# GpSimd's memsets and one weight split moved behind the layer norm in a six-block transformer kernel

## What is computed

```python
def _layernorm(x, axis=-1, eps=1e-05):
    m = jnp.mean(x, axis=axis, keepdims=True)
    v = jnp.var(x, axis=axis, keepdims=True)
    return (x - m) / jnp.sqrt(v + eps)
...
    x = x + _L0_xattn_ref(_layernorm(x, axis=-1), ctx_4096, L0_xattn_Wq, L0_xattn_Wk, L0_xattn_Wv, L0_xattn_Wo)
    x = x + _L0_attn_ref(_layernorm(x, axis=-1), L0_attn_w_q, L0_attn_w_k, L0_attn_w_v, L0_attn_w_out)
    x = x + _L0_ffn_ref(_layernorm(x, axis=-1), L0_ffn_route_w, L0_ffn_A, L0_ffn_Bw)
    x = x + _L1_xattn_ref(_layernorm(x, axis=-1), ctx_4096, ctx_4096, L1_xattn_Wq, L1_xattn_Wk, L1_xattn_Wv, L1_xattn_Wo)
    x = x + _L1_attn_ref(_layernorm(x, axis=-1), L1_attn_Wq, L1_attn_Wk, L1_attn_Wv, L1_attn_Wo, L1_attn_cos, L1_attn_sin)
    x = x + _L1_ffn_ref(_layernorm(x, axis=-1), L1_ffn_rmsnorm_weight, L1_ffn_Wg, L1_ffn_Wu, L1_ffn_Wd)
```

## Time and profile before

| what | value |
|---|---|
| median of three runs | 2087.39 us |
| the profiled execution's own time | 2098.17 us |
| its span | 2096.8 us |
| TensorE busy | 1927.6 us (92%) |
| VectorE busy | 1292.1 us (62%) |
| ScalarE busy | 860.1 us (41%) |
| GpSimd busy | 546.6 us (26%) |
| mean DMA rate | 124 GB/s |

### The profile page before, as it was taken

How to read it: one execution, slowest core, us unless ns; L and a number is a source line. 1 busy time by engine, 2 the same in 40 slices (tenths; PEclk the granted TensorE clock), 3 DMA queues, 4 the chain that set the end, 5 groups by cost and what they waited for, 6 DMA issues and landing times.

```text
span 2096.8 us, 29638 instructions
## 1 busy us (share of the span) xinstructions
PE 1927.6 (92%) x11932; PEld 1414.5 (67%) x11932; DVE 1292.1 (62%) x1608; ACT 860.1 (41%) x1409; POOL 546.6 (26%) x264
## 2 busy tenths in 40 slices
PE   7899999999997999999998996989999999978977
PEld 5799999999996778787776874623333333366833
DVE  3445454454444788889976755757777774266465
ACT  2211111111113666665664451146777777535421
POOL 0000000000001555564510001046777777410000
PEclk9999999999998999999999998879999999999889
DMA  5543433343326656666625426523434320135052
GB/s 178 169 119 94 126 98 113 99 124 92 86 76 169 212 189 199 189 204 207 223 89 152 161 72 180 112 75 79 99 79 91 87 59 1 41 121 219 1 190 74
DMA packets 154808, 259.30 MB, mean 124 GB/s; under 512 B 36477, under 2 KB 102321, under 8 KB 147505
## 3 DMA queue, kind: packets, MB, share of 16 engines
q1 hardware_dynamic: 154673, 257.42, 41.3%
HBM read 192.39 MB, written 61.76 MB: 121 GB/s over the span
## 4 chain that ended last, share of the span: by engine, by line
PE 81%; DVE 10%; ACT 3%; DMA 2%; issue 2%; SPq 0%; POOL 0%; ACTq 0%; DVEq 0%
PE psum L475 10%; PE psum L1720 7%; PE psum L1737 5%; PE psum L456 4%; PE psum L458 4%; PE psum L457 4%; PE psum L443 3%; PE psum L285 3%; PE psum L286 3%; PE psum L287 3%; PE psum L1753 3%; PE psum L816 3%; DVE top L1913 3%; PE psum L817 3%; PE psum L818 3%; PE psum L831 3%
## 5 line engine op out<-in xcount | busy, mean ns | idle before, releaser
L1913 DVE TENSOR_REDUCE top<-psum 128x4 f32<-128x2048 f32 (+1 forms) x146 | 294.0, 2026 | 103.2 <-PE psum L1701 102.9
L1983 POOL TENSOR_TENSOR added<-probs_f 128x1024 f32<-128x1024 f32 x126 | 299.1, 2376 | 181.5 <-ACT probs_f L1838 133.7
L1838 ACT ACTIVATE probs_f<-psum 128x512 f32<-128x512 f32 x512 | 278.5, 594 | 142.0 <-PE psum L1720 129.7
L608 DVE TENSOR_REDUCE top<-psum 128x2 f32<-128x512 f32 x272 | 186.5, 692 | 198.0 <-PE psum L443 197.8
L907 DVE TENSOR_TENSOR probs_low<-probs,probs_high 128x1024 fp32r<-128x1024 f32 x136 | 197.7, 1458 | 77.7 <-ACT probs L870 77.5
L869 ACT ACTIVATE probs_high<-psum 128x1024 fp32r<-128x1024 f32 x136 | 139.9, 1029 | 164.1 <-PE psum L818 151.6
L1720 PE MATMUL psum<-q_rows,k_rows 97*128 97x512 f32 x512 | 197.7, 462 | 3.1 <-DMA q_rows<-t_high 2.4
L1720 PEld LDWEIGHTS psum<-q_rows,k_rows 97*128 97x128 f32 x512 | 80.9, 191 | 174.1 <-ACT probs_f L1838 159.0
L456 PE MATMUL psum<-c_high,w_high 128*128 128x256 f32 (+1 forms) x672 | 190.7, 284 | 3.2 <-issue 3.2
L457 PE MATMUL psum<-c_low,w_high 128*128 128x256 f32 (+1 forms) x672 | 190.6, 284 | 0.0
L458 PE MATMUL psum<-c_high,w_low 128*128 128x256 f32 (+1 forms) x672 | 190.5, 284 | 0.0
(11 more groups left out here) (359 smaller groups left out, 3820.2 us busy)
## 6 DMA issues: line engine op xcount, KB each, us to landing
wf_rows<-in_ffn_w_dram SPq DMA_DIRECT2D x42, 512.0 KB, 4.4
staged<-in_ctxT_dram SPq DMA_DIRECT2D x32, 512.0 KB, 4.7
k_four<-k_high SPq DMA_DIRECT2D x128, 128.0 KB, 3.4
wf_rows<-in_ffn_w_dram SPq DMA_DIRECT2D x8, 1376.0 KB, 7.9
q_dram<-wf_turned SPq DMA_DIRECT2D x42, 256.0 KB, 2.3
gate_up<-q_dram SPq DMA_DIRECT2D x10, 1024.0 KB, 8.1
value_high<-v_high SPq DMA_DIRECT2D x32, 256.0 KB, 3.7
value_low<-v_low SPq DMA_DIRECT2D x32, 256.0 KB, 4.6
```

The source lines that it names most:

```text
L608: dve.tensor_reduce(top0[:, r0:r0 + 2, n], psum[:, bank, :].rearrange("p (i n) -> p i n", i=2), AX_X, ALU.max).then_inc(*b.bank_read.up())
L1838: act.activation(probs[:, n % 6, half * BANK:(half + 1) * BANK], psum[:, half, :], ACT.Exp, scale=scale).then_inc(*f.exped.up())
L1913: dve.tensor_reduce(top1[:, first:end, t, chunk], psum[:, MAXIMA + first:MAXIMA + end, :], AX_X, ALU.max).then_inc(*f.max_read.up())
L1983: pool.tensor_tensor(added[pair % 4][:], probs[:, n % 6, :], probs[:, (n + 1) % 6, :], ALU.add).then_inc(*f.added.up())
```

## The change

dve_output leaves out its split at the last unit. In both causal stages VectorE makes that split directly behind the layer norm instead, ahead of the low parts of xnT: unit 3 of the query weights (unit 19 of the stream) in d, unit 1 (57) in g. These are the only two places where the left-out step did something. GpSimd's memsets in the causal stages and in the second cross attention wait for the norm's end (xn_set) in place of the last addition to x (x_added). No instruction is added or removed.

```diff
--- before.py
+++ after.py
@@ -311,12 +311,13 @@
                     act_split(u0 + u + ahead)
 
         def dve_output(u0, per, ahead, upto, banks):
+
             for u in range(2 * per):
                 if u % per == per - 1:
                     dve.wait_ge(*s.unit_read.at(u0 + u + 1))
                     for t in range(TT):
                         dve_add_to_x(u // per, t, banks[TT * (u // per) + t])
-                if u0 + u + ahead < upto:
+                if u0 + u + ahead < upto and u < 2 * per - 1:
                     dve_split(u0 + u + ahead)
 
 
@@ -1403,6 +1404,7 @@
                     done.then_inc(*f.o_set.up())
 
                 dve_layernorm(norm, [xn[:, t, :] for t in range(TT)])
+                dve_split(u_q + (3 if ahead == 4 else 1))
                 for i in range(KT // 2):
                     dve.wait_ge(*f.xnT_high_set.at(i + 1))
                     dve.tensor_tensor(xnT_low[:, 2 * i:2 * i + 2, :], bank_pair(4 + i),
@@ -1469,7 +1471,7 @@
 
             def gpsimd_program():
                 wait_pool()
-                pool.wait_ge(*s.x_added.at(before))
+                pool.wait_ge(*s.xn_set.at(norm))
                 pool.memset(qz[:], 0.0).then_inc(*f.zeroed.up())
 
             def sync_program():
@@ -1970,7 +1972,7 @@
                     pool.tensor_tensor(oT_low[:, kv, :], o_raw[:], oT_high[:, kv, :].bitcast(F32),
                                        ALU.subtract).then_inc(*f.o_split.up())
 
-                pool.wait_ge(*s.x_added.at(before))
+                pool.wait_ge(*s.xn_set.at(4))
                 pool.memset(ones[:], 1.0).then_inc(*f.ones_set.up())
                 for k in k_rows:
                     pool.wait_ge(*f.ones_set.now())
```

## The result

| | before | changed |
|---|---|---|
| median of six runs, us | 2088.04 | 2077.64 |
| lowest to highest | 2086.55 to 2093.22 | 2074.64 to 2079.01 |
| the profiled execution, us | 2098.17 | 2078.95 |

The ratio is 0.9944, with a 95% interval of 0.9930 to 0.9958: 11.7 us faster, between 8.8 and 14.6 (the medians by themselves lie 10.4 apart). The forecast was 13.2 us and 2074.2.

What follows compares the result with a forecast made beforehand. TensorE bounds the kernel (81% of the chain), idling behind three norms; memsets' 11.17 us and splits' 2.00 make 13.16, rounded to 13.2 off 2087.39: 2074.2 us, range 2071.0 to 2079.5.

Steps and rivals of the forecast that it cites:

- The stalls: In three norms, L172 and L188 held by GpSimd memsets; moving these removes 1.35, 5.06 and 4.76 us, 11.17 together.
- the sum of 13.16 us: Excess from last L303 to first transpose: 2.34 us in d, 5.06 in second cross attention, 5.76 in g.
- four ends: L172 (three norms) and L188 (second cross attention) each end with a GpSimd memset, agreeing within 0.03 us.
- The division of the sum: Of the gain at the norms, 11.17 us came from the memsets and 2.00 from the splits in d and g.
- The moved split: Behind the norm in d and g, 1.21 us fits VectorE's idle 1.84, leaving 0.6; cost nothing.
- The first rival: In d and g the memset holds the moved split, giving back up to 2.9 and 6.3 us: 2083.4; chance 0.04.
- The mask: In g it lands later, ScalarE waits 2 us at L1286; covered with 1.7 us to spare, cost zero.
- The fourth rival: In d and g a very late mask makes ScalarE keep high parts from TensorE: 2091.9 or slower; chance 0.02.
- The panels of the query projection: In the second cross attention two weight panels land before TensorE's transposes end, covered by 0.7 us.
- The second rival: Query projection panels land late, taking at most the second cross attention's 5.06 us: 2079.3; chance 0.05.
- The clock: TensorE still restarts at half clock behind the three norms, after idle times of about 6.15 us; net cost taken as zero.
- The range's 3 and 4 us: Allowance for TensorE's half clock behind restarts: about 3 us below the forecast and 4 above.

Runs made afterwards that it cites:

- the last kernel: Changed kernel plus tables ahead of the last panel, one projection split ahead of the additions, 25 unread matmuls before each norm's wait, 45 before feed-forward: 2070.83 us, ratio 0.9879.
- the two kernels with fillers: Changed kernel with unread TensorE matmuls before the norms' waits: 40 each, ratio 0.9964; 25 each, 45 before feed-forward, plus two order edits, ratio 0.9879.

## Why the prediction was right, point by point

- The stalls. L172 and L188 at 0.17 us in all norms, 4.06 or 4.07 us from L303 to L208 in each stage: the sum of 13.16 us stands in the trace as 13.17. That the memset is the cause was argued from four ends and is now shown: the memsets alone bring 5.07 us in the second cross attention and 1.34 and 4.77 in the others, the split alone lengthens L172 to the same end.
- The division of the sum. The prediction gave 2.00 us to the splits as a part of its own. Alone they are worth nothing. It should have read the split as a step in front of a fixed end: where a wait for something else lies behind it, taking it away only lengthens the wait.
- The moved split. 1.22 us beside the memset, with 0.70 us of VectorE's wait left, as worked out (0.6). The first rival fell; the run with a reading GpSimd operation shows when it would have been right.
- The mask. A new wait of ScalarE of 3.26 us in g, against the 2 worked out, since the mask landed 6.1 us after its issue and not 4.5. TensorE asked for its fourth unit 12.4 us behind its restart, not 11.5, because it ran at half clock for longer, so the margin was 1.2 us, against 1.7. The term stays at nothing. The fourth rival fell.
- The panels of the query projection. No wait in the changed kernel (0.69, released by ScalarE). The second rival was near all the same: with 1.7 us off the transposes and the LoRA stage 2.9 us shorter, so that the panels go out later against the norm, the panel is what TensorE waits for, by 3.15.
- The clock. "The new idle times are all about 6.15 us" was off for the second cross attention, 5.14, because TensorE's last product there ends later against VectorE's additions; the rows of before would have said so (10.35 less 5.06 is 5.29). In the second profile of the changed kernel it is 6.21, with the LoRA stage ahead of it 2.2 us shorter and less of it at half clock, so this time too depends on the execution. It did restart at half clock in all three. The range's 3 and 4 us were sized by one restart; the larger part of the scatter lies further on, at the attention's pauses: 28 to 47 us at half clock in the second cross attention in these profiles, of which the first 10 us behind the restart hold 9 at most. That this didn't carry the time out of the range was in part luck; nothing in the prediction priced it. The profiled time was put at 2085, with the first profile's surplus of 10.8 us kept; it was 2078.95, since that surplus belonged to one execution.
- The size. 13.2 us foretold, 11.7 and 10.9 measured in two comparisons, with intervals that hold 13.2. If the missing 2 us are real, no run here says where they are; the late mask is ruled out by the traces of g, where 1.2 us were to spare.

## What to carry to other kernels

When a tiny VectorE instruction is many times longer than its twin elsewhere (here up to 29 times), lay GpSimd's timeline beside it and compare ends. Put GpSimd's long memsets where VectorE runs tensor_tensors or reads PSUM, and don't count on cutting them up unless GpSimd waits between the pieces. A term of a sum that lies ahead of a wait with a fixed end is worth nothing until that wait is gone; test parts alone before writing a gain to each. And when idle time before TensorE has been cut as far as it will go, the half-rate restart behind it may be the larger price: fillers that end before the wait left the restart at full clock, fillers that end after it cost their overrun. Then look at the clock further on: in the last kernel one stage was 5.3 us longer, for a cause that is open.

## What the runs showed of the hardware that was not expected

- Memsets on GpSimd that follow one another without a semaphore wait hold VectorE's tensor_scalar as one: 5.20 us for L172 behind eight pieces of 0.95 us. With a signal and a wait between the pieces: 0.98.
- A tensor_tensor with both operands in SBUF is untouched by a GpSimd memset (1.22 us) and held for the rest of a GpSimd tensor_scalar (6.69 us).
- The same pauses of TensorE, 1.13 and 0.20 us inside otherwise dense work, are followed by 10 us at half clock in one execution and by none in another, 4.7 us of a 133 us stage.
- With the clock kept up at the restart of the second cross attention, the half clock that begins some 50 us further on lasted 24 and 31 us in the two kernels with fillers, against 17 in the changed kernel. In both profiles of the kernel before, which restarted at half, it lasted 31, so the cause is open.
